# Expert layer of a 64-expert kernel: quads of experts with down products by token in four column groups, slots laid out expert by expert

## What is computed

```
shared_out = _swiglu(x, shared_w1, shared_w2)
gates = softmax(x @ wg.T)                       # 64 experts
w_topk, idx_topk = top_k(gates, 8)              # normalised to sum 1
buf = zeros((64, 160, H)).at[se, rank].set(x[st], mode='drop')   # CAPACITY = 160
h = einsum('ech,efh->ecf', buf, expert_w1)      # up: 128 -> 2 x 384
x1, x2 = split(h, 2)
out = einsum('ecf,ehf->ech', x1 * silu(x2), expert_w2)           # down: 384 -> 128
combined = zeros((T, H)).at[st].add(y * sw)
x = layernorm(x + shared_out + combined)
```

## Time and profile before

| what | us |
|---|---|
| median of the runs | 649.73 |
| lowest and highest of 3 | 646.76, 653.32 |
| span of the profiled execution | 688.8 |
| from the first expert product to the last transpose | 146 to 365 |
| first and last scatter | 175.7, 371.7 |

### The profile page before, as it was taken

The page is one execution under the profiler, slowest core; times in us unless marked ns, Lnnn a source line. Parts: engine busy times, 40 slices in busy tenths (PEclk is TensorE's granted clock), DMA queues, the critical chain, the costliest instruction groups (busy, mean ns, idle before and its releaser), DMA issues.

```text
span 688.8 us, 11455 instructions
## 1 busy us (share of the span) xinstructions
PE 593.3 (86%) x3947; PEld 493.7 (72%) x3947; DVE 431.1 (63%) x1330; ACT 247.9 (36%) x472; POOL 312.6 (45%) x313
## 2 busy tenths in 40 slices
PE   6999887669898897879879789799999999999881
PEld 5678655568898787879875767587777877787650
DVE  4588788953333234243433868687778777887793
ACT  3133254003222223222334034443444435444754
POOL 4765203876666666666552134322343223423431
PEclk9999998879999999999999989999999999999997
DMA  8970001227767667676715900000100000000001
GB/s 297 414 308 16 25 23 29 53 64 235 243 216 242 203 223 230 219 229 215 241 48 196 409 27 0 1 12 6 31 11 4 15 27 4 15 16 1 1 0 61
DMA packets 29565, 79.44 MB, mean 115 GB/s; under 512 B 7104, under 2 KB 12096, under 8 KB 29264
## 3 DMA queue, kind: packets, MB, share of 16 engines
q1 hardware_dynamic: 23088, 65.69, 27.1%
q0 software_dynamic: 6432, 13.16, 6.5%
HBM read 62.60 MB, written 16.25 MB: 114 GB/s over the span
## 4 chain that ended last, share of the span: by engine, by line
PE 66%; DVE 18%; issue 6%; another core or an unknown queue 3%; ACT 3%; POOL 1%; DMA 0%; DVEq 0%; ACTq 0%; SPq 0%; POOLq 0%
PE bank L799 12%; PE bank L980 8%; PE bank L968 8%; PE bank L809 7%; PE bank L903 4%; PE bank L559 4%; PE bank L924 3%; DVE arena L1756 2%; PE bank L878 2%; PE bank L894 2%; PE bank L944 2%; PE bank L915 2%; PE bank L591 2%; DVE hidden L1842 2%
## 5 line engine op out<-in xcount | busy, mean ns | idle before, releaser
L280 POOL TENSOR_TENSOR rstd<-veps,minus_half 128x4 f32<-128x4 f32 x52 | 54.0, 1038 | 231.2 <-DVE veps L273 225.7
L799 PE MATMUL bank<-hidden,ring 128*128 128x160 f32 x768 | 120.2, 307 | 3.3 <-DVE hidden L1830 2.5
L799 PEld LDWEIGHTS bank<-hidden,ring 128*128 128x128 f32 x768 | 111.0, 197 | 4.2 <-DVE hidden L1830 2.9
L1842 DVE TENSOR_TENSOR hidden<-bank,hidden 128x480 f32<-128x480 f32 x64 | 41.9, 654 | 113.8 <-ACT hidden L1227 64.8
L1460 POOL DMA_INDIRECT returned_rows<-x1t,scatter_all x80 | 79.8, 997 | 61.2 <-PE bank L799 26.0
L809 PE MATMUL bank<-hidden,ring 128*128 128x160 f32 x384 | 66.9, 311 | 28.6 <-DVE hidden L1842 21.4
L809 PEld LDWEIGHTS bank<-hidden,ring 128*128 128x128 f32 x384 | 56.5, 194 | 34.0 <-DVE hidden L1842 25.2
L1227 ACT ACTIVATE hidden<-bank 128x480 f32<-128x480 f32 x64 | 37.3, 582 | 107.3 <-PE bank L799 65.3
L1453 POOL DMA_INDIRECT arena<-dispatch_rows,gather_all x50 | 53.1, 1063 | 33.2 <-DVE scatter_all L1788 14.1
L1292 ACT ACTIVATE arena<-bank,layer_cols 128x512 f32<-128x512 f32 x64 | 43.9, 687 | 60.7 <-PE bank L968 60.7
L980 PE MATMUL bank<-ring,arena 128*128 128x128 f32 x512 | 59.9, 275 | 1.4 <-issue 1.4
(11 more groups left out here) (231 smaller groups left out, 1097.3 us busy)
## 6 DMA issues: line engine op xcount, KB each, us to landing
ring<-in_ew SPq DMA_DIRECT2D x64, 576.0 KB
returned_rows<-zeros SPq DMA_DIRECT2D x16, 512.0 KB, 15.6
arena<-returned_rows SPq DMA_DIRECT2D x6, 512.0 KB, 13.4
hidden<-returned_rows SPq DMA_DIRECT2D x4, 512.0 KB
ring<-returned_rows SPq DMA_DIRECT2D x4, 512.0 KB
ring<-in_l1w SPq DMA_DIRECT2D x8, 256.0 KB, 2.6
returned_rows<-x1t,scatter_all POOLq DMA_INDIRECT x80
shared<-in_xr SPq DMA_DIRECT2D x1, 1024.0 KB, 8.0
```

Of the source, the lines that this page charges most:

```text
L280: pool.tensor_tensor(rstd[:, s, :], veps[:, s, :], minus_half[:], ALU.pow).then_inc(sem(f"rstd{which}_ready"), 1)
L799: mm = pe.matmul(bank[2 * (n % 2) + part][:, CAP * f:CAP * f + CAP], ring[:, n % RING, P * (FB * part + f):P * (FB * part + f) + P], E["xt ...
L1842: v.tensor_tensor(E["prod"][:, n % 2, :], bank[2 * (n % 2)][:, 0:FB * CAP], E["silu"][:, n % 2, :], ALU.mult).then_inc(sem("prod_g_ready"), 1)
```

## The change

Slots become expert-major: a partition stands for (expert of the quad, slot part). `find_slots` now computes for each of the four experts its own 32 partitions, from 32 stationary and 10 moving columns, into a column group of its own; `indices` reads the bank directly, without mask and sum, and tells gathers and scatters apart (`gather_ready`, `scatter_ready`).

Down products are done by quad and by token: `expert_results` takes 32 tokens of an expert's products as the stationary operand and the 128 columns of down weights as the moving one, for the four experts in four column groups, three or two slot blocks at a time (c = 0, 1). The result is by token at once, so `turn_results`, `keep_result` and `yt` go. The silu is written into `prod` itself, of which there are 8; up products have three pairs of banks (HIDDEN = 3).

SyncE loads up weights by expert (384 KB) when the expert eight places back has its up products done, and down weights by quad (768 KB, 1536 B a row) when the results two quads back are done. GpSimd issues 40 gathers ahead, then scatters and gathers by turns, and waits for data alone. There are four `back` buffers.

The diff, cut to its core:

```diff
-    c[:, C_EXP:C_EXP + EG] = (r[:, None] % EG) == np.arange(EG)[None, :]
+    c[:, C_EXP:C_EXP + EG] = (r[:, None] // RA) == np.arange(EG)[None, :]
...
-        GOT, BACK = 8, 3
+        GOT, BACK = 8, 4
...
+        PROD = 2 * EG
+        E = carve([("prod", (PROD, FB * CAP), F32)], TILES * RA * EG // 2 * EG)
+        E.update(carve([("back", (BACK, RB, D), F32)], NEG * TILES * RA * EG // 2))
+        E["xt"] = flat_hidden[:, 0:2 * EG * CAP].rearrange("p (u e s) -> p u e s", u=2, e=EG)
...
+            def load_up(n):
+                sp.dma_start(ring[:, n % RING, 0:2 * FFN], ew[n][:, 0:2 * FFN]).then_inc(
+                    sem(f"expert_then_tile_in{n % RING}"), 16)
+
+            def load_down(Q):
+                at = EG * Q % RING
+                sp.dma_start(ring[:, at:at + EG, 2 * FFN:], ew[EG * Q:EG * Q + EG].rearrange("n p c -> p n c")[:, :, 2 * FFN:]
+                             ).then_inc(sem(f"down_in{Q % 2}"), 16)
...
             for n in range(RING, NE):
-                sp.wait_ge(sem("expert_mm"), n - RING + LAG + 1)
-                sp.dma_start(ring[:, n % RING, :], ew[n]).then_inc(sem(f"expert_then_tile_in{n % RING}"), 16)
+                sp.wait_ge(sem("expert_mm"), n - RING + 1)
+                load_up(n)
+                if n % EG == 2 and n // EG >= 3:
+                    sp.wait_ge(sem("result_mm"), 2 * (n // EG - 2))
+                    load_down(n // EG - 1)
...
-                        at = 2 * RB * EG * (2 * k + u)
-                        lo = EG * (2 * q + u)
+                        Q, at = 2 * q + u, 2 * RB * (2 * k + u)
                         for i in range(TILES):
-                            mm = pe.matmul(slot_bank(call)[:, at:at + 2 * RB * EG], a16[:, 2 * q + u, i, :],
-                                           b16[:, :, i, lo:lo + EG], start=(i == 0), stop=(i == TILES - 1))
+                            for e in range(EG):
+                                mm = pe.matmul(slot_bank(call)[RA * e:RA * e + RA, at:at + 2 * RB], a16[:, Q, i, :, e],
+                                               b16[:, :, i, EG * Q + e], start=(i == 0), stop=(i == TILES - 1))
...
             def expert_hidden(n):
+                Q, j = n // EG, n % EG
+                if j == 0:
+                    pe.wait_ge(sem("xt_read"), 2 * (Q + 1))
+                if n >= HIDDEN:
+                    pe.wait_ge(sem("prod_g_ready"), n - HIDDEN + 1)
+                pe.wait_ge(sem(f"expert_then_tile_in{n % RING}"), 16 * (n // RING + 1))
...
+            def expert_results(Q, c):
+                if c == 0:
+                    pe.wait_ge(sem("prod_g_ready"), EG * (Q + 1))
+                    pe.wait_ge(sem(f"down_in{Q % 2}"), 16 * (Q // 2 + 1))
+                if Q + 2 < NEG:
+                    pe.wait_ge(sem("xt_read"), 2 * (Q + 2) + c + 1)
+                else:
+                    pe.wait_ge(sem("back_read"), 2 * (Q - 1) + c + 1)
+                for k, b in enumerate(REST if c else FIRST):
+                    for f in range(FB):
+                        for e in range(EG):
+                            n = EG * Q + e
+                            mm = pe.matmul(bank[6 if c else 7][RA * e:RA * e + RA, P * k:P * k + P],
+                                           E["prod"][:, n % PROD, CAP * f + RA * b:CAP * f + RA * b + RA],
+                                           ring[:, n % RING, P * (2 * FB + f):P * (2 * FB + f) + P],
+                                           start=(f == 0), stop=(f == FB - 1))
+                mm.then_inc(sem("result_mm"), 1)
...
-                if n >= LAG:
-                    done = expert_result(n - LAG)
...
+                if j < 2 and Q + 1 < NEG:
+                    turn_inputs(Q + 1, j)
+                elif j >= 2 and Q >= 1:
+                    expert_results(Q - 1, j - 2)
+                expert_hidden(n)
             for c in range(2):
-                turn_results(NEG - 1, c).then_inc(sem("last_turned"), 1)
+                expert_results(NEG - 1, c)
...
+            for n in range(NE):
+                act.wait_ge(sem("expert_mm"), n + 1)
+                act.activation(E["prod"][:, n % PROD, :], bank[2 * (n % HIDDEN) + 1][:, 0:FB * CAP], ACT.Silu).then_inc(
                     sem("silu_ready"), 1)
...
+            for Q in range(GOT):
+                for b in range(RB):
+                    gather_block(Q, b)
             pool.wait_ge(sem("zeroed"), 16 * TOK * TOPK // (8 * P))
...
+            for Q in range(NEG):
                 for b in range(RB):
                     scatter_block(Q, b)
+                    if Q + GOT < NEG:
+                        gather_block(Q + GOT, b)
...
-                v.tensor_tensor(picked[:, 0:n], slot_bank(call)[:, 0:2 * RB * EG * n].rearrange(
...
+                found = slot_bank(call)[:, 0:2 * RB * n].rearrange("p (u t b) -> p u t b", u=n, t=2)
+                tok1, place1 = found[:, :, 0, :], found[:, :, 1, :]
...
+                v.tensor_scalar(gather_all[:, qs], tok1, -1.0, 0.0, ALU.add, ALU.max).then_inc(sem("gather_ready"), 1)
```

162 lines of the change are left out of this document (38 added, 124 removed).

## The result

The changed kernel takes 660.62 us (median of 4 runs, 658.91 to 662.28), the kernel before 651.53 us in the same session (4 runs, 646.76 to 653.57). The ratio is 1.0164, 95% interval 1.0121 to 1.0207: slower by about 9 us, where 647 us was forecast. The time lies inside the range that takes in the rivals (610 to 665), outside the forecast's own (640 to 655), on the wrong side of no change, and at rival B's number (660).

What follows compares the result with a forecast made beforehand. TensorE's expert work was taken as the bound, GpSimd's indirect DMAs second. TensorE 142.6 + 180 + 7 = 330, GpSimd 331, against 332.6: -2 us, and -1 for the tail, gave 647 us; own range 640 to 655, with rivals 610 to 665.

Steps and rivals of the forecast that it cites:

- rival B: Slots on TensorE: small matmuls keep 0.025 us each, deciding from about 0.012; +10, 660 us; chance 0.22.
- The slots' term: Slots on TensorE: four column groups run abreast, so 1024 small matmuls add 0; +14 us kept as bound.
- VectorE's index steps: Slot indices on VectorE: without mask and sum, 2.3 us of earlier start.
- A quad of experts: Expert stage on TensorE: 11.3 us a quad against 10.9, bounds 10.6 and 12.2, down products 4.2 with switches.
- The experts as a whole: Expert stage on TensorE: 16 quads take 180 us, bounds 170 and 195.
- The forecast of -2: End of the scatters: 331 us against 332.6 in ordinary runs of the kernel before, with all behind shifting along.
- GpSimd's bound of 331: Indirect DMAs on GpSimd: 40 gathers issued by 174.8, the remaining 120 at 1.30 us end at 331.
- The 39.1 us: Span of 688.8 us over the median of 649.73: taken as lateness of the recorded execution in the expert stage.
- rival A: Expert stage: the recorded waits are the kernel's own also in ordinary runs; -37, 612 us; chance 0.22.
- C: Rival on down products: the column groups don't run four abreast; +40, 687 us, in series +144; chance 0.09.

Runs made afterwards that it cites:

- e2: The kernel before with the changed slots alone (1024 small products, indices read from the bank); 661.74 us, ratio 1.0170.
- e6: The changed kernel with each of the 1024 slot products moving 40 columns instead of 10; 662.49 us, ratio 1.0188.
- e4: The kernel before, unchanged, recorded once more; 649.19 us (one run), span 647.4.
- e14: The kernel before, unchanged, recorded a third time; 651.51 us (one run).
- e12: The kernel before with the 1 MB in_xr transfer issued later; 649.24 us, ratio 0.9997.
- e9: The changed kernel with 256 slot products from the old table, turned expert-major behind the next call's products, tables before indices; 652.63 us, ratio 1.0048.
- e7: The changed kernel with a quad's down products issued expert by expert instead of four experts in turn; 781.34 us (one run).
- e13: The changed kernel, unchanged, recorded once more; 660.31 us, ratio 1.0149.
- e1: The changed kernel with 256 slot products again, from a table written expert-major; 670.32 us, ratio 1.0299.

## Why the prediction was wrong, step by step

- **The slots' term, 0 taken and +14 kept as bound.** This is the step that failed. "I take 0, by L591, whose loads and matmuls overlapped": they do overlap in bursts (128 products in 1.27 us, 0.010 us each, below the 0.012 from which B decides), but a burst is at most 167 products long, and mostly 128. Over a group a product costs 3.8/128 = 0.030 us, rival B's price of 0.025 and more. Between ranks and transposes the change needs 45.3 us instead of 35.7: +9.6 us, and e2 has +8.8 with nothing else changed. L591 was 4 instructions in a microsecond and could say nothing of a supply that is used up after 128. The nearest row for that was one I had read for another end: L755 itself, 128 in 3.76 us, the same number of instructions per microsecond.
- **B's mechanism** was a price per product on TensorE. Its place and result (transposes +14, 660 us) came out, but its cause is not the one given: the bursts, e6 and the queue's loads show a supply of instructions. The number was partly luck: of the +13.1 at the transposes only 9.6 are the slots', the rest was there at the ranks. Its 4.8 us of delay in the first two calls did not come, since they start from instructions already there.
- **VectorE's index steps** without mask and sum: the change's calls are shorter, but TensorE's gaps hide it. Nothing gained.
- **A quad of experts, 11.3 us forecast, bounds 10.6 and 12.2.** 170.35 to 181.37 is 11.02 us. The down products take 3.55 us by their spacing (busy 3.69), against 4.2 taken. The switches are seen in the up products beside them, 12 of which last 1.63 us before a transpose:

```profile
168.63 1.79 PE L799 MATMUL bank<-hidden,ring 128*128 128x160 f32 x12
175.73 1.90 PE L799 MATMUL bank<-hidden,ring 128*128 128x160 f32 x12
177.46 0.49 PE L787 MATMUL bank<-consts,small 128*128 128x128 f32 x3
177.79 1.80 PE L799 MATMUL bank<-hidden,ring 128*128 128x160 f32 x12
179.42 0.38 PE L787 MATMUL bank<-consts,small 128*128 128x128 f32 x2
```

  168.63 to 170.35 is 1.72, 172.45 to 174.28 is 1.83, 175.73 to 177.46 is 1.73: 0.1 us at each change between whole-array and grouped products, 0.4 us a quad. So 4.35 us of down products and transposes became 4.1, the changes took 0.4, and a quad is 11.0 instead of 10.9: that TensorE's work gets no less was forecast.
- **The experts as a whole.** Forecast 180 from the first up product to the last results; 157.76 to 336.06 is 178.3. From the transposes it is 180.7, where the kernel before, recorded in order, needs 181 to 185; and 187 to the last scatter, where that one needs 189 to 192. Part of this gain of 2 to 5 us is the clock: behind the transposes it is granted 0.50 for 6.3 us in the changed record, but for 8.1, 8.8 and 6.6 in e4, e14 and e12, and e4 has 3.4 us more at 304. What is left is some 2 us (an estimate, half of each stretch taken off), and roughly fits waits of 3.7 to 4.6 us that became 1.7 and a last scatter 1.0 us closer behind the last results, less 0.14 us a quad. The forecast of -2 met it by luck, since it was made of GpSimd's end and of a start 2.3 us earlier.
- **GpSimd's bound of 331** did not bind in the change: its cadence is 1.29 us, but it waited for VectorE's results before the last five scatters, which follow TensorE's.

```profile
336.32 0.98 POOL L1444 DMA_INDIRECT returned_rows<-arena,scatter_all  x1 [2.44 <-DVE arena L1823]
```

  In e9, which starts its experts 11 us earlier, it ends at 331.5 and waits for results 2.8 us in all, so there the two bounds nearly meet, as the prediction had them.
- **The 39.1 us** were read rightly (e4), and A was given too much (0.22) for a story that one record told; C (0.09) is refuted by 0.24 us a set and by e7.
- **What was not in the sum**: the rest of the kernel takes 1 to 3 us longer behind the change (316 to 317 against 313 to 315). It is not that the last quad's results end nearer to the last scatter (6.5 us against 7.5) and TensorE's own 17 us of shared expert begin later: TensorE then waits less for the returned rows (1.44 us against 2.48 in e14), and its sum over the rows from `ring` starts 14.1 us behind the last scatter in both. The clock is part of it. It is granted 0.50 in the last 9 to 12 us of every record, and in stretches before: the rest is 313.3 with 3.4 us at 0.50 behind the scatters (e4), 314.4 with 6.8 (e12), 315.1 with 10.2 (e14), and in the change 316.0 with 6.8 (e13) and 317.3 with 10.2. About 2 us are left, without a cause.

In numbers, e13 against e14: ranks +1.2, slots +9.8, experts -3.0, rest +0.9: 8.8 us of span (658.5 against 649.7).

The Trainium skill, "TensorE: Matmul & The Clock Gate" (Back-to-back issue gap), says that starts never lie closer than about 25 ns. The trace disagrees for bursts of small products in four column groups (1.27/128 = 10 ns). The sustained pace, 0.030 us, does not go against it, but the gaps make that pace. By that rule alone the forecast would have been rival B's 660.

## What to carry to other kernels

Splitting a product into column groups multiplies instructions, and in the slots TensorE was fed some 67 of them per microsecond (a load and a product are two). Where pieces are shorter than 0.03 us each, and there are more than the 128 to 167 in a row that passed at once here, count the pieces and not their columns. Gaps with "issue" behind regular numbers of equal instructions, together with the instruction queue's loads, are its mark. Before reading waits from one record whose span is far from the median, record the kernel again: the second record (e4) took away rival A and the stray 32 us.

## What was unexpected in the hardware

- **A like pace of instructions in three places.** Slots in groups 256 instructions in 3.8 us, whole-array slots 256 in 3.63 us (e9), down products 240 in 3.48 us: 67, 71 and 69 per us. Only the first shows gaps, so only there is the supply shown to be the cause. e14 has 96 whole-array products, 192 instructions, in 2.56 us, 75 per us, so the likeness may be chance.
- **Narrow products alone**: 32 x 128 float32 by itself 0.095 us a pass (e7), in four groups by turns 0.030 us each.
- **VectorE's fp16 comparison** of 128x2048 takes 1.15 us with the repeated operand outside and 2.2 us with it innermost (e1).
- **A stray record**: 688.8 us of span for a kernel whose other records have 647.4 and 649.7, with signals late by up to 2.9 us in the expert stage.
